# Normalisation and softmax division from VectorE to GpSimd, and an expert unit's two matmul groups in one step

## The reference

```python
x = x + attn_a(layernorm(x), Wq, Wk, Wv)      # 16 heads of 8; softmax over all keys, causal mask AFTER it
x = x + ffn(layernorm(x), router_w, expert_bias, w1, w2, w3, sw1, sw2, sw3)
x = x + attn_b(layernorm(x), w_qkv, w_out, b_out)   # RoPE, 16 heads of 8, no mask
x = x + ffn(layernorm(x), ...)
```

```python
def _layernorm(x, axis=-1, eps=1e-05):
    m = jnp.mean(x, axis=axis, keepdims=True)
    v = jnp.var(x, axis=axis, keepdims=True)
    return (x - m) / jnp.sqrt(v + eps)
```

## Time and profile before

| | us |
|---|---|
| three runs | 1900.91, 1904.55, 1908.56 |
| median | 1904.55 |
| the profiled execution, its own time | 1906.13 |
| its span, first to last instruction | 1904.1 |

### The profile page before, as it was taken

The page is one execution under the profiler, slowest core; times in us unless marked ns, Lnnn a source line. Parts: engine busy times, 40 slices in busy tenths (PEclk is TensorE's granted clock), DMA queues, the critical chain, the costliest instruction groups (busy, mean ns, idle before and its releaser), DMA issues.

```text
span 1904.1 us, 44343 instructions
## 1 busy us (share of the span) xinstructions
PE 1852.5 (97%) x16816; PEld 885.6 (47%) x16816; DVE 1566.8 (82%) x3083; ACT 1432.9 (75%) x2840; POOL 883.0 (46%) x1210
## 2 busy tenths in 40 slices
PE   6999999999999999999999999999999999999997
PEld 3444444444444444444444444444444444444446
DVE  4988998888888888988889888988888888788826
ACT  3388887777777777777788787778877877777782
POOL 6142333455655567555643434435334454544520
PEclk8599998999999999999999999999999999999999
DMA  7111110000100101001100101001100010000000
GB/s 254 35 68 68 58 42 3 1 28 27 52 2 35 35 24 47 2 35 35 35 35 2 51 25 62 2 2 52 40 19 8 2 30 29 24 2 8 7 2 12
DMA packets 39380, 61.91 MB, mean 33 GB/s; under 512 B 5632, under 2 KB 20608, under 8 KB 39040
## 3 DMA queue, kind: packets, MB, share of 16 engines
q1 hardware_dynamic: 39168, 59.08, 9.5%
HBM read 30.74 MB, written 27.26 MB: 30 GB/s over the span
## 4 chain that ended last, share of the span: by engine, by line
PE 86%; DVE 9%; ACT 2%; issue 2%; POOL 1%; DMA 0%; DVEq 0%; ACTq 0%; POOLq 0%
PE ps_sum L1212 28%; PE ps_banks L1178 20%; PE ps_banks L1232 11%; PE ps_banks L1153 9%; PE ps_banks L1253 8%; DVE negmax L940 5%; PE ps_banks L1124 2%; PE ps_banks L1167 2%; PE ps_banks L1131 1%; DVE xn L958 1%; PE ps_banks L1110 1%; PE ps_banks L1223 1%; ACT sums L810 1%; PE ps_banks L1138 1%; PE ps_banks L1160 1%
## 5 line engine op out<-in xcount | busy, mean ns | idle before, releaser
L940 DVE TENSOR_REDUCE negmax<-ps_banks 128x1 f32<-128x512 f32 x2048 | 1280.7, 680 | 196.0 <-PE ps_banks L1153 192.4
L803 ACT ACTIVATE probs<-ps_banks 128x512 f32<-128x512 f32 x2048 | 1085.7, 604 | 195.2 <-PE ps_banks L1178 182.5
L1153 PE MATMUL ps_banks<-kx,qx 24*128 24x512 f32 x2048 | 650.0, 507 | 7.4 <-DVE hid L991 3.6
L1178 PE MATMUL ps_banks<-qx,kx 26*128 26x512 f32 x2048 | 528.6, 500 | 3.5 <-DVE hid L991 1.8
L1212 PE MATMUL ps_sum<-probs,vg 128*9 128x256 f32 (+1 forms) x6144 | 463.8, 374 | 6.8 <-ACT sums L810 6.0
L1178 PEld LDWEIGHTS ps_banks<-qx,kx 26*128 26x128 f32 x2048 | 197.3, 183 | 374.1 <-issue 168.1
L692 POOL TENSOR_SCALAR scaled<-scaled,gates 128x128 f32<-128x128 f32 x516 | 182.9, 372 | 283.1 <-ACT scaled L854 244.2
L1153 PEld LDWEIGHTS ps_banks<-kx,qx 24*128 24x128 f32 x2048 | 260.4, 185 | 103.6 <-ACT probs L803 55.1
L664 POOL TENSOR_TENSOR pdiag<-probs,causal 128x512 f32<-128x512 f32 x128 | 163.5, 1278 | 173.3 <-ACT probs L803 172.4
L680 POOL TENSOR_TENSOR hid<-hid,first 128x512 f32<-128x512 f32 x129 | 164.9, 1278 | 125.8 <-DVE hid L991 121.4
L1212 PE MATMUL ps_sum<-probs,w 128*9 128x256 f32 (+1 forms) x2560 | 187.7, 365 | 2.0 <-ACT sums L810 1.3
(11 more groups left out here) (104 smaller groups left out, 1289.0 us busy)
## 6 DMA issues: line engine op xcount, KB each, us to landing
qk_rows<-limbs SPq DMA_DIRECT2D x36, 512.0 KB, 3.5
qx<-qk_rows SPq DMA_DIRECT2D x128, 96.0 KB
kx<-qk_rows SPq DMA_DIRECT2D x128, 96.0 KB
qx<-mlimbs SPq DMA_DIRECT2D x512, 2.0 KB
qk_rows<-prod_c SPq DMA_DIRECT2D x8, 512.0 KB, 3.7
qk_rows<-prod_s SPq DMA_DIRECT2D x4, 512.0 KB, 2.7
out_dram<-x SPq DMA_DIRECT2D x8, 256.0 KB, 2.3
x<-in_x SPq DMA_DIRECT2D x3, 512.0 KB, 5.9
```

The costliest lines, as they stand in the source:

```text
L803: act.activation(m.probs[:, blk % PROB_SLOTS, EXP_HEADS[k], :], bank, ACT.Exp, scale=SCALE).then_inc(s.freed[SCALAR], 1)
L940: dve.tensor_reduce(m.negmax[:, unit // UNITS % 2, half, col:col + 1], bank, AX.X, ALU.max, negate=True).then_inc(s.freed[VECTOR], 1)
L1153: pe.matmul(bank_of(("scores", unit, k)), m.qx[rows, n % SLOTS, tile * P:(tile + 1) * P], m.kx[rows, n % SLOTS, half * CHUNK:(half + 1) * ...
L1178: pe.matmul(bank, m.kx[rows, n % SLOTS, j * P:(j + 1) * P], m.qx[rows, n % SLOTS, half * CHUNK:(half + 1) * CHUNK], start=True, stop=True) ...
```

## The change

It moves "apply" from DVE to POOL, where it follows the power; the copy of the means and its two waits go, and POOL makes the negated means with one small operation more. The placing of "apply" goes from step 4 or 5 to step 3 after the statistics. The division's multiply moves to POOL, ahead of the addition of the heads; only the reciprocal stays on DVE; both now stand at a new item "finish", two steps behind "sums". "h3" moves to the step of its "h1", directly behind it, and DVE's multiply to a new item "product" one step later; POOL's "hidden" follows in that step. The counts of DVE's readings are kept by where the reading now stands (`freed`). Two starts of later work move by 2 and 3 steps. In `ended` "product" stands directly behind "h3".

```diff
+H3_AT = 0
...
 def projected_a(c, at):
-    return staged(at, (0, ("stats", 0, c)), (1, ("moments", 0, c)), (4, ("apply", 0, c)), (6, ("turn", 0, c)),
+    return staged(at, (0, ("stats", 0, c)), (1, ("moments", 0, c)), (3, ("apply", 0, c)), (6, ("turn", 0, c)),
...
 def prepared(layer, c, at):
-    return staged(at, (0, ("stats", layer, c)), (1, ("moments", layer, c)), (5, ("apply", layer, c)),
+    return staged(at, (0, ("stats", layer, c)), (1, ("moments", layer, c)), (3, ("apply", layer, c)),
                   (8, ("turn", layer, c)), (11, ("logits", layer, c)))
...
 def feed_forward(k, at):
-    return staged(at, (0, ("h1", k)), (3, ("h3", k)), (4, ("hidden", k)), (7, ("y", k)), (9, ("gate", k)))
+    return staged(at, (0, ("h1", k)), (H3_AT, ("h3", k)), (H3_AT + 1, ("product", k)), (H3_AT + 1, ("hidden", k)),
+                  (7, ("y", k)), (9, ("gate", k)))
...
-        more, at = routed(1, b * HALVES, HALVES, (b + 1) * HALVES * of_chunk + 11)
+        more, at = routed(1, b * HALVES, HALVES, (b + 1) * HALVES * of_chunk + 13)
...
-        at = (CHUNKS + c + 1) * of_chunk + 9
+        at = (CHUNKS + c + 1) * of_chunk + 12
...
-        add_side(side, {(p + 1) * UNITS + 2 * WEIGH_LAG + 3: [("sums", p)]})
+        add_side(side, staged((p + 1) * UNITS + 2 * WEIGH_LAG + 3, (0, ("sums", p)), (2, ("finish", p))))
...
+        self.read = {SCALAR: {}, VECTOR: {}}
+        for item in plan:
+            held = ("h3", *item[1:]) if item[0] == "product" else item
+            if held[0] in READER and item[0] != "h3":
+                read = self.read[READER[held[0]]]
+                read[held] = len(read)
...
     def deviations(layer, c):
         i = counts.nth("stats", layer, c)
-        pool.wait_ge(s.stats_kept, i + 1)
+        pool.wait_ge(s.stats_done, (i + 1) * CT)
...
+        pool.tensor_scalar(m.lower[:, i % 2, :], m.mv[:, i % 2, :, 0], -1.0, 0.0, ALU.mult, ALU.add
+                           ).then_inc(s.shifted, 1)
+        pool.wait_ge(s.shifted, 2 * (i + 1))
         pool.tensor_tensor(m.rstd[:, c * CT:(c + 1) * CT], m.shifted[:, i % 2, :], m.expo[:, :], ALU.pow
                            ).then_inc(s.rstd_done, 1)
 
+    def apply(layer, c):
+        n, i = counts.nth("apply", layer, c), counts.nth("stats", layer, c)
+        pool.wait_ge(s.rstd_done, i + 1)
+        if n >= 2:
+            turned = [item for item in counts.turns if item[0] == "turn"][n - 2]
+            pool.wait_ge(s.filled[SCALAR], counts.use(*turned) + 1)
+        for t in range(CT):
+            tile = c * CT + t
+            last = pool.tensor_scalar(m.xn[:, n % 2, t * P:(t + 1) * P], m.x[:, tile_cols(tile)],
+                                      m.lower[:, i % 2, t:t + 1], m.rstd[:, tile:tile + 1], ALU.add, ALU.mult)
+        last.then_inc(s.xn_done, 1)
...
-    def add_heads(p):
+    def finish(p):
...
+        pool.wait_ge(s.inverted, p + 1)
+        pool.tensor_tensor(dst, src[:, :, :, 0:HD], m.recip[:, turn, :, :].to_broadcast([P, CT, GH, HD]), ALU.mult
+                           ).then_inc(s.finished, 1)
+        if masked_after(n):
...
+            pool.tensor_tensor(cols, cols, dst.rearrange("p t h d -> p t (h d)"), ALU.add).then_inc(s.headed, 1)
...
     def moments(layer, c):
...
-        dve.wait_ge(s.stats_done, (i + 1) * CT)
-        applied = [item for item in counts.kind["apply"] if item[2] == c and item[1] < layer]
-        if applied:
-            dve.wait_ge(s.xn_done, counts.nth(*applied[-1]) + 1)
-        dve.tensor_copy(m.mean[:, c * CT:(c + 1) * CT], m.mv[:, i % 2, :, 0]).then_inc(s.stats_kept, 1)
...
-        elif kind == "h3":
+        elif kind == "product":
             gated_hidden(*of)
...
         holder = counts.held_by(*item)
         if holder:
-            pe.wait_ge(s.freed[READER[holder[0]]], counts.use(*holder) + 1)
+            pe.wait_ge(s.freed[READER[holder[0]]], counts.freed(*holder) + 1)
```

More of the change, by code:

```diff
@@ L266, in ended @@
     items = [("weigh", blk, part) for blk in range(last - WEIGH_LAG, last) for part in range(2)]
-    items += [("copy", p), ("sums", p)]
+    items += [("copy", p), ("sums", p), ("finish", p)]
     units = list(range(done, 2 * LAYER_UNITS))
@@ L275, in ended @@
         add_side(side, {1 + i * (late - 1) // len(stages): stage})
-    items += [("h1", done), ("h3", done)]
+    items += [("h1", done), ("h3", done), ("product", done)]
     for i, k in enumerate(units):
@@ L279, in ended @@
         if i + 1 < len(units):
-            items += [("h1", k + 1), ("h3", k + 1)]
+            items += [("h1", k + 1), ("h3", k + 1), ("product", k + 1)]
         items.append(("mix", k))
@@ L332, in use, with freed @@
         return self.uses[READER[item[0]]][item]
+    def freed(self, *item):
+        return self.read[READER[item[0]]][item]
     def bank(self, *item):
@@ L381, in allocate @@
     m.shifted = sb("shifted", [P, 2, CT])
-    m.mean = sb("mean", [P, TILES])
+    m.lower = sb("lower", [P, 2, CT])
     m.rstd = sb("rstd", [P, TILES])
@@ L629, in low_of_x @@
         t = counts.turns[("turn", layer, c)]
-        pool.wait_ge(s.freed[SCALAR], counts.use("turn", layer, c) + 1)
+        pool.wait_ge(s.freed[SCALAR], counts.freed("turn", layer, c) + 1)
         pool.tensor_tensor(m.x_lo[:, slot, :], m.xt[:, t % 2, :], m.x_hi[:, slot, :].bitcast(F32),
@@ L648, in split_max @@
     def split_max(p):
-        pool.wait_ge(s.freed[SCALAR], counts.use("maxima", p) + 1)
+        pool.wait_ge(s.freed[SCALAR], counts.freed("maxima", p) + 1)
         if p:
@@ L658, in mask @@
         d = counts.nth("mask", blk)
-        pool.wait_ge(s.freed[SCALAR], counts.use("exp", blk, GH - 1) + 1)
+        pool.wait_ge(s.freed[SCALAR], counts.freed("exp", blk, GH - 1) + 1)
         if d >= 2:
@@ L700, in add_scaled @@
         x = m.x[:, chunk_cols(c)]
-        pool.wait_ge(s.freed[SCALAR], counts.use(*item) + 1)
+        pool.wait_ge(s.freed[SCALAR], counts.freed(*item) + 1)
         if i:
@@ L732, in pool_program @@
             mask(*of)
-        elif kind == "sums" and masked_after(place(*of)[0]):
-            add_heads(*of)
+        elif kind == "apply":
+            apply(*of)
+        elif kind == "finish":
+            finish(*of)
         elif kind == "hidden":
@@ L943, in combine @@
     def combine(p):
-        dve.wait_ge(s.freed[VECTOR], counts.use("scores", (p + 1) * UNITS - 1, 1) + 1)
+        dve.wait_ge(s.freed[VECTOR], counts.freed("scores", (p + 1) * UNITS - 1, 1) + 1)
         if p:
@@ L948, in combine, with invert @@
                           ).then_inc(s.combined, 1)
[L950 to L964, removed]
+    def invert(p):
         turn = slice(p % 2 * CT, (p % 2 + 1) * CT)
-        dve.wait_ge(s.freed[SCALAR], counts.use("sums", p) + 1)
+        dve.wait_ge(s.freed[SCALAR], counts.freed("sums", p) + 1)
+        if p >= 2:
+            dve.wait_ge(s.finished, p - 1)
         src = m.sums[:, p % 2 * CHUNK:(p % 2 + 1) * CHUNK].rearrange("p (t h r) -> p t h r", t=CT, h=GH)
         dve.reciprocal(m.recip[:, turn, :, :], src[:, :, :, HD:HD + 1]).then_inc(s.inverted, 1)
[L969 to L980, removed]
     def gated_hidden(k):
@@ L1028, in chain @@
             last = ("logits", layer, c + width - 1)
-            dve.wait_ge(s.freed[SCALAR], counts.use(*last) + 1)
+            dve.wait_ge(s.freed[SCALAR], counts.freed(*last) + 1)
         if k == 2:
@@ L1121, in queries_keys @@
         t = counts.turns[("turn", layer, c)]
-        pe.wait_ge(s.freed[SCALAR], counts.use("turn", layer, c) + 1)
+        pe.wait_ge(s.freed[SCALAR], counts.freed("turn", layer, c) + 1)
         pe.wait_ge(s.b_weights, DMA * 6)
@@ L1128, in query_or_key @@
         t = counts.turns[("turn", 0, c)]
-        pe.wait_ge(s.freed[SCALAR], counts.use("turn", 0, c) + 1)
+        pe.wait_ge(s.freed[SCALAR], counts.freed("turn", 0, c) + 1)
         pe.wait_ge(s.a_weights, DMA * 3)
@@ L1198, in weigh @@
         if part == 0:
-            pe.wait_ge(s.freed[SCALAR], counts.use("exp", blk, GH - 1) + 1)
+            pe.wait_ge(s.freed[SCALAR], counts.freed("exp", blk, GH - 1) + 1)
             if j == 0 and blk:
@@ L1248, in mix_experts @@
         else:
-            pe.wait_ge(s.freed[VECTOR], counts.use("h3", k) + 1)
+            pe.wait_ge(s.freed[VECTOR], counts.freed("h3", k) + 1)
         pe.wait_ge(s.other_weights, DMA * 6)
```

49 lines of the change are left out of this document (26 added, 23 removed).

## The result

| | before | after |
|---|---|---|
| median, measured together (4 runs each) | 1905.66 us | 2142.01 us (2131.2 to 2153.58) |
| ratio after / before, 95% interval | | 1.124, 1.118 to 1.131 |
| span of the profiled execution | 1904.1 us | 2129.4 us (its own time 2131.2) |
| mean granted TensorE clock, share of 2.4 GHz | 0.976 | 0.885 |

The change makes the kernel 12.4% slower, 236 us, where 71 us were forecast. The page after, of the fastest of the four executions (the other three had mean clocks of 0.873 to 0.880): busy times, the clock in 40 slices, and two groups (busy, mean ns, idle ahead and its releaser).

A forecast was written before the change was run, and what follows sets the result against it. PE and DVE hand banks back and forth, neither the bound alone. 1906.1 + 103 (ring) + 4 (start and tail) - 31 - 4 (DVE's relief) = 1978, given as 1976 us against the runs' median; range 1888 to 2018 us.

The forecast's parts named there:

- The ring's term: Expert units: a scores matmul waits for h3's bank until DVE's late product; 77 us at 7 steps, 26 at 5.
- the merged burst: h3 directly behind h1 on PE: 0.21 us less for each of 129 units, 27 us of PE time.
- PE's view: Scores matmul behind a burst: 0.87 us lost, 0.21 saved, 0.66 us more a unit.
- DVE's view: Round of 7 steps counted by DVE's maxima: 11.6 us against 10.5 without diagonals, 1.1 us more.
- A round of 7 steps takes near 12 us: Sign that the forecast is right, in the expert units; the round read before took 11.16 us.
- DVE is behind in about half of a round, so I take half, 31 us: 300 to 1850 us: of 61.6 us of work leaving DVE, half shortens the time; bounds 0 and 62.
- the lone price: DVE's moved tiles priced without the excess: applies at 0.338 us, divides at 0.291, relief 48 us, half of it 24.
- goes with the operations: DVE's moved tiles: their excess time is waiting for POOL and leaves with them, so the 61.6 us stand.
- rival C: POOL becomes late: 24 applied chunks and 55 divides each hold a weigh half a microsecond; 2016 us, chance 0.07.
- A: Rival: the ring's wait lies where PE waits anyway, and the merged burst saves 27 us; 1848 us, chance 0.16.
- B: Rival: loss and relief cancel, 0.3 us a unit of the stall stays; 1914 us against 1906, chance 0.09.
- D: Rival: DVE's product would stand ahead of the burst's own maxima; no chance of its own, counted inside A.

The follow-up runs named there:

- E2: The changed kernel with DVE's product in the step of h1 and h3, ahead of that step's maxima, hidden one step later; 1878.41 us, ratio 0.985.
- E5: The changed kernel with h3 back at step 3 and product and hidden at step 4, so a late product without adjacent groups; 2160.32 us, ratio 1.136.
- E1: The changed kernel with h3 and product back at step 3 and hidden at step 4, leaving only the moves to POOL; 1902.59 us, ratio 1.001.
- E3: The kernel before with h3 at step 0, product and hidden at step 1, normalisation and division left on DVE; 2178.71 us, ratio 1.144.
- E6: The kernel before, normalisation and division on DVE, with h3 and product in the step of h1, hidden one later; 1926.02 us, ratio 1.012.

## Why the prediction was right and wrong

**The direction and the place were right.** "That matmul waits for h3's bank", and "DVE gives it back only behind the two maxima of the burst's own step": PE waits on the product over a hundred times (117), 1.09 us each against "some 0.9", and the times within the round agree to 0.14 us. E2 takes the mechanism away by moving one instruction, E5 brings it about alone.

**The ring's term was about right in size.** Forecast 103 us net of the merged burst (77 + 26). Measured: 114 us of wait by the rounds, less 24 for the merge (E1 to E2, 1902.6 to 1878.4; forecast 27), is 90 net. At 7 steps the rounds show 0.87 us of wait, which is the figure of PE's view ahead of its saving, and DVE's view was too high; at 5 steps they show 1.06 where 0.87 was taken.

**The step that failed: TensorE's clock has no term.** The sum prices every matmul at the duration of the earlier trace rows, as if PE could be made to wait 1 us in each round and keep its clock. The rows of before gave no occasion to see it, since 300 to 1850 us stand at 0.99; but they showed the lower level too, 0.93 in the stretch from 68 to 300 us, so that the price could have been asked for. Measured: mean 0.885, 392 us more at the lower level than in E2, some 141 us by the rounds. It is the largest single part of the miss: added to the forecast it alone gives 1976 + 141 = 2117. "A round of 7 steps takes near 12 us" fell too, but partly because the round it was read from was a short one: the 7-step rounds are 12.6 us long on average before and 14.4 after.
The Trainium skill (TensorE: Matmul & The Clock Gate, "A second HAM failure mode: psum-queue depth-cycling") has a case of this kind, in a bf16 kernel: micro-idles between groups of matmuls, from cycling through PSUM banks, make the clock go down and up again and again. The trace agrees: 0.82 us busy of 2, then 0.50. By the Trainium skill (TensorE: Matmul & The Clock Gate, "Terms") the penalty is about half of the time at the lower level; that would be an estimate of 196 us for the 392 us. The rounds give 0.36 and not 0.5, and the measurement decides.

**A second term was mis-sized: "DVE is behind in about half of a round, so I take half, 31 us".** That is, with 4 us ahead of 300 us, 35 us of relief. With the groups apart it is 0 (E1, 1902.6 against 1903.7): DVE's busy time did fall, by 69 us over the span, but being late in part of a round was not being the bound. In the order of the change itself it is 37 us (E3 to after), nearly the forecast's figure, but by luck: some 27 of them come from the clock, which the forecast left out, and 10 from DVE's time. With the product in time it is 48 us (E6 to E2), 32 of them the clock's. The term depends on the rest of the change, and the forecast gave it one value.
DVE's busy time itself fell by less than the earlier trace rows had it: in 300 to 1850 us from 1283.4 to 1232.9 us (E1), 50.5 against 61.6, nearer to the 48 that the lone price gave. Where the rest went is seen in one group of the stretch, first of the kernel before, then of E1:

```profile
L947 DVE TENSOR_TENSOR lowest<-negmax 128x16 f32<-128x16 f32 x53 | 18.3, 345 | 1.8
```
```profile
L980 DVE TENSOR_TENSOR lowest<-negmax 128x16 f32<-128x16 f32 x53 | 25.1, 474 | 1.8
```

A tile with two operands from SBUF takes 474 ns where it took 345, 7 us in all, while the maxima, read from PSUM, stay (680 and 681 ns). By the Trainium skill (SBUF — State Buffer, "Who interferes with whom") DVE and GpSimd exclude each other at a shared pair of ports; the trace agrees, but what the forecast made of it, that the excess "goes with the operations", was wrong in good part: of the 13.6 us of excess (61.6 - 48) 11 came back. POOL is busy 833 and not 770 us there, so more of DVE's other tiles can meet it; that this is what slowed them is inferred and not tested.

**POOL.** An apply takes 449 ns (0.37 taken, the bound of 0.46 held), a divide 408 (0.46 taken). No wait of a weigh for POOL stands in the trace after, and E3 has the whole loss without the moves: rival C falls. In E2, where the rest runs faster, weighs wait for a mask 9 times, 8.0 us. By the Trainium skill (GPSIMD Engine Reference, "Engine selection") a two-input tile is about twice as slow there; 408 ns stand against DVE's 291 to 518, 1.4 times at most.

**Start.** PE's wait for the first normalised chunks grew from 16.9 to 23.2 us: 6 us, for which +4 with a bound of 6 was given.

**The new sum.** 1905.7 + 0 for relief and start (E1) - 24 for the merge (E2) + 114 at the ring + 141 for the clock = 2137 us against 2142 measured. The last two are found separately, as a line's constant and slope, so that they add up to the difference is a check on them; they are read from one execution of each kernel.

**Rivals.** A and B fall, as the wait is some 0.9 us a unit. D falls in the kernel after; it is E2, and there A's direction holds, with 25 us gained (1903.7 to 1878.4) where 58 were reckoned (1906 to 1848).

**What stays open:** why E5, with the same waits of PE, has less time at the lower level than the kernel after, why a given wait is or is not followed by a fall, and what in E6 lets the clock down.

## What to carry to other kernels

In a ring of banks shared by all engines a reading belongs in the step of its writing: moved one step later, behind two maxima of the same engine, it held the bank up to the seventh item behind it and cost 264 us, with no work added. When a change makes a dense PE wait, look first at the granted clock, and price the wait twice, for itself and for what runs at the lower level behind it. And relief of an engine that is late only in part of a round has no value of its own: it was worth 0, 37 and 48 us in three orders of work, so try it in the order that is to stay.

## What was not expected of the hardware

- Behind a wait of 1.18 us (PE busy 0.82 of 2 us) the clock stood at 0.50, and an attention step took 1.70 us and not 0.98. This did not follow each wait: behind the one of 1.05 us at 776 us the matmul rows stayed at 0.50 us, those of the higher level.
- Matmuls of zeros, put where PE waits, made the kernel 84 and 100 us faster though they are work added.
- An us at the lower clock cost 0.36 us, not half of one, in a kernel that PE and DVE bound by turns.
- POOL's 128x128 apply with two scalars per partition takes 449 ns, longer than its divide of two inputs (408 ns).
